# Image pipeline with attention: two buffers of normalised sums, three tiles divided after turning, and another order of maxima, projection and loads

## The reference

```python
# layer 0, per image and channel
x = x + relu(-median(x))                       # median over the 16384 pixels
y = relu(upfirdn2d(x, lpf, up=2))              # 7 taps, zero padded
x = upfirdn2d(y, lpf, down=2)
# layer 1
spec = rfft2(x)                                # gate from |spec|: two 1x1 maps, gelu, sigmoid
xf = x + irfft2(spec * gate)
q = xf @ q_w + q_b                             # 4 heads of 16, 16384 queries
k, v = keys and values of two strided convolutions of xf (8x8: 256 keys, 16x16: 64 keys),
       layer norm, kv map, v by a 3x3 depthwise convolution
out = softmax(q k^T / 4) v                     # 320 keys
result = out @ proj_w + proj_b + x
```

## Time and profile before

| | us |
|---|---|
| median of 3 runs | 10953.36 (10936.6 to 10957.42) |
| the profiled execution's own time | 10947.25 |
| its span, from the first to the last instruction | 10945.9 |
| busy: PE, weight loads, DVE, ACT, POOL | 9935.8, 4884.1, 8640.6, 7155.3, 5880.3 |

### The profile page before, as it was taken

How to read it: one execution, slowest core, us unless ns; L and a number is a source line. 1 busy time by engine, 2 the same in 40 slices (tenths; PEclk the granted TensorE clock), 3 DMA queues, 4 the chain that set the end, 5 groups by cost and what they waited for, 6 DMA issues and landing times. The chain is left out here.

```text
span 10945.9 us, 199054 instructions
## 1 busy us (share of the span) xinstructions
PE 9935.8 (91%) x69001; PEld 4884.1 (45%) x69001; DVE 8640.6 (79%) x14529; ACT 7155.3 (65%) x12301; POOL 5880.3 (54%) x10577
## 2 busy tenths in 40 slices
PE   1998998989989899899989999899898998989989
PEld 1534535344353543535435353453534435354353
DVE  7887778878788777878777788777887878877787
ACT  5766667666666766667666676666667666676665
POOL 1374463745637365472744737446374553836547
PEclk9999999999999999999999999999999999999999
DMA  2031231312314032140322303123131331413214
GB/s 61 29 77 51 56 90 30 79 40 65 81 33 90 27 76 70 41 90 36 73 55 51 96 23 80 46 59 87 32 79 37 68 79 34 90 33 72 67 44 102
DMA packets 330611, 664.69 MB, mean 61 GB/s; under 512 B 95624, under 2 KB 241160, under 8 KB 308048
## 3 DMA queue, kind: packets, MB, share of 16 engines
q1 hardware_dynamic: 329552, 651.29, 25.1%
HBM read 232.53 MB, written 71.30 MB: 28 GB/s over the span
## 5 line engine op out<-in xcount | busy, mean ns | idle before, releaser
L1350 ACT ACTIVATE R<-ps 128x512 f32<-128x512 f32 x5120 | 2874.0, 593 | 1460.9 <-PE ps L826 1020.6
L1117 DVE TENSOR_REDUCE R<-ps 128x2 f32<-128x640 f32 x3840 | 3028.3, 818 | 725.7 <-PE ps L805 682.1
L269 ACT ACTIVATE R<-R,st 128x1475 bf16<-128x1475 f32 (+2 forms) x1326 | 2014.4, 1519 | 441.5 <-DVE st L343 416.3
L332 DVE TENSOR_SCALAR_CACHE_REDUCE R<-R,st 128x1255 bf16<-128x1255 f32 (+2 forms) x1326 | 2015.1, 1520 | 19.5 <-DVE st L343 0.2
L805 PE MATMUL ps<-KST,R 96*128 96x320 bf16 x7680 | 1683.2, 300 | 42.9 <-DMA R<-R 21.6
L851 PE MATMUL ps<-R 128*32 128x512 f32 x12288 | 1670.1, 617 | 0.0
L826 PE MATMUL ps<-R,KST 104*128 104x512 bf16 x4096 | 1583.2, 389 | 11.4 <-ACT R L1350 6.8
L1447 POOL TENSOR_TENSOR R<-R 128x256 f32<-128x256 f32 x1440 | 1056.9, 734 | 115.2
L1451 POOL TENSOR_TENSOR R<-R 128x256 f32<-128x256 f32 x1440 | 1050.2, 729 | 119.9
L805 PEld LDWEIGHTS ps<-KST,R 96*128 96x128 bf16 x7680 | 703.0, 98 | 752.6 <-DVE R L1117 280.0
L826 PEld LDWEIGHTS ps<-R,KST 104*128 104x128 bf16 x4096 | 394.6, 97 | 1043.8 <-ACT R L1350 749.6
(11 more groups left out here) (226 smaller groups left out, 19536.4 us busy)
## 6 DMA issues: line engine op xcount, KB each, us to landing
R<-R SPq DMA_DIRECT2D x3072, 64.0 KB, 2.4
R<-xh_in SPq DMA_DIRECT2D x136, 512.0 KB, 4.5
out_dram<-Z SPq DMA_DIRECT2D x68, 1024.0 KB, 3.9
R<-Wk SPq DMA_DIRECT2D x960, 64.0 KB, 2.0
Wk<-Wk SPq DMA_DIRECT2D x960, 64.0 KB, 2.0
R<-xa_in SPq DMA_DIRECT2D x36, 1024.0 KB, 10.1
R<-xb_in SPq DMA_DIRECT2D x36, 1024.0 KB, 11.7
R<-sr_in SPq DMA_DIRECT2D x32, 1024.0 KB, 5.0
```

The costliest lines, as they stand in the source:

```text
L269: e.activation(junka[:, 2047:2048] if k == LONE else junka[:, 0:o2 - o1], xc[:, o1:o2], ACT.Sign, bias=mid, scale=-1.0, accum_out=ca[i]).t ...
L332: e.tensor_scalar(junk[:, 0:o1 - o0], xc[:, o0:o1], mid, None, ALU.is_le, ALU.add, accum_out=cv[i]).then_inc(md_cv, 1)
L1117: e.tensor_reduce(MX[(4 * u + s4) % 2][:, blk_, h0:h0 + 2], ps[:, 2 + 2 * bq:4 + 2 * bq, 0:320], axis=AX.X, op=ALU.max).then_inc(mx, 1)
L1350: e.activation(PB[:, t % 2, w, :], ps[:, w % 2, :], ACT.Exp).then_inc(ex, 1)
```

## The change

- STAGES moves the stages from slots 2 and 6 to slots 4 and 8, or from 2 to 4.
- The normalised sums get two buffers NO[0] and NO[1] of their own. `normalise` runs for tiles 0 to 28, and waits only for its own last result and for the projection of the tile two back. The turned sums ON and OX move to another place.
- TURNED = 3: tiles 29, 30 and 31 are divided after turning. The turning of tile 29 lies inside tile 31 (turn after slot 1, turn_back after slot 6).
- `project_out` is for tile t - 4, in slot 0; `rest` follows in slot 2.
- `split_max` is in slot 2 of the tile in whose slot 3 `lay_max` turns the maxima (they were in slot 8 of the tile before, and slot 0).
- SP: lay_out comes first, for tile t - 2; `load_next` is cut in two parts, in tiles 28 and 29; two loads of a unit come ahead of lay_max and the others behind it; the units 2 and 3 are loaded by eight DMAs in a tile, one unit after the other.
- VectorE's reductions of the next image (`largest`, L305) move to the slots 4 and 6 of tile 31.

```diff
@@ -21,11 +21,13 @@
 WAITS = 4
 AHEAD = 2
 WEIGHS = (2, 4, 8)
-STAGES = {(0, 2): (1, 0, 6), (0, 6): (1, 1, 6), (1, 2): (1, 2, 6), (1, 6): (1, 3, 6),
-          **{(8 * g - 12 + j, 2): (g, j, 6) for g in (2, 3) for j in range(4)}}
+STAGES = {(0, 4): (1, 0, 6), (0, 8): (1, 1, 6), (1, 4): (1, 2, 6), (1, 8): (1, 3, 6),
+          **{(8 * g - 12 + j, 4): (g, j, 6) for g in (2, 3) for j in range(4)}}
 ADDS = {17: (0,), 19: (1,), 21: (2,), 23: (3,), 25: (4,), 27: (5,), 31: (6, 7)}
 FIRST = [(0, i) for i in range(11)] + [(1, 0), (1, 1)] + [(0, i) for i in range(11, 16)] + [(1, 2), (1, 3)]
-LOADS = {u: 2 if u == 2 else 4 * u - 8 for u in range(2, 8)}
+LOADS = {**{3 * u - 4 + i: (u, 8 * i, 8 * i + 8) for u in (2, 3) for i in range(3)},
+         **{4 * u - 8 + i: (u, 6 * i, 6 * i + 6) for u in range(4, 8) for i in range(4)}}
+TURNED = 3
 NP = 3
 CUTS = [HALF * i // NP for i in range(NP + 1)]
 LONE = 20
@@ -154,7 +156,8 @@
         OR = [W[:, 512 * i:512 * i + 512] for i in range(2)]
         XO = [W[:, 1024 + 256 * i:1280 + 256 * i] for i in range(2)]
         XD = [R2[:, 1024 + 256 * i:1280 + 256 * i] for i in range(2)]
-        XI, XN2, ON, OX = (R2[:, 1536 + 256 * i:1792 + 256 * i] for i in range(4))
+        XI, XN2, *NO = (R2[:, 1536 + 256 * i:1792 + 256 * i] for i in range(4))
+        ON, OX = W[:, 1536:1792], W[:, 1792:2048]
         RD = [R2[:, 2640 + 16 * i:2656 + 16 * i] for i in range(2)]
         RS = [W[:, 1536 + 512 * i:2048 + 512 * i] for i in range(2)]
...
 
 
 
-        def load_next(e, it, half, landed=None):
+        def load_next(e, it, half, landed=None, part=None):
             src = (xa, xb)[half][bass.ds(it, 1), :, :, :].rearrange("a c t n -> (a t) c n")
+            a, b = (0, 4096) if part is None else (2048 * part, 2048 * part + 2048)
             for t in range(2):
-                e.dma_start(xc[64 * t:64 * t + 64, 4096 * half:4096 * half + 4096], src[t, :, :]).then_inc(landed or in_xc[half], 16)
+                e.dma_start(xc[64 * t:64 * t + 64, 4096 * half + a:4096 * half + b], src[t, :, a:b]).then_inc(landed or in_xc[half], 16)
 
         def load_image(e, it, k):
...
                 for i in range(2):
-                    op = e.matmul(ps[:, 6, 128 * i:128 * i + 128], lhsT=XN2[:, 128 * i:128 * i + 128], rhs=c("pw"),
+                    op = e.matmul(ps[:, 6, 128 * i:128 * i + 128], lhsT=NO[t % 2][:, 128 * i:128 * i + 128], rhs=c("pw"),
                                   start=True, stop=True)
                 op.then_inc(po_ps, 1)
...
@@ -870,13 +874,13 @@
                 op.then_inc(den_ps, 1)
 
             def turn_back(t):
-                e.wait_ge(od, t - NT + 3)
+                e.wait_ge(od, t - NT + TURNED + 1)
                 for i in range(2):
                     op = e.transpose(ps[:, 4 + t % 2, 128 * i:128 * i + 128], ON[:, 128 * i:128 * i + 128], c("ident"))
                 op.then_inc(ot_ps, 1)
 
             def project_back(t):
-                e.wait_ge(ox, t - NT + 3)
+                e.wait_ge(ox, t - NT + TURNED + 1)
                 e.wait_ge(*b6[0])
                 for i in range(2):
                     op = e.matmul(ps[:, 6, 128 * i:128 * i + 128], lhsT=OX[:, 128 * i:128 * i + 128], rhs=c("pw"),
@@ -897,19 +901,24 @@
                         values()
                     if w < 8 and ahead < NT:
                         maxima(ahead // 4, ahead % 4, w)
-                    if w == (0 if t else 4) and t + AHEAD - 1 < NT:
+                    if w == 0 and t > 3:
+                        project_out(t - 4)
+                    if w == 3 and t + AHEAD - 1 < NT:
                         lay_max(t + AHEAD - 1)
                     if w in WEIGHS and t:
                         weigh(t - 1, WEIGHS.index(w))
-                    if w == 5 and t > 2:
-                        project_out(t - 3)
                     if (t, w) in STAGES:
                         stage(*STAGES[t, w])
-            e.wait_ge(mx, 8 * NT - 16)
+                    if t == NT - 1 and w == 1:
+                        e.wait_ge(mx, 8 * NT - 16)
+                        turn(NT - 3)
+                    if t == NT - 1 and w == 6:
+                        turn_back(NT - 3)
+            project_out(NT - 4)
             turn(NT - 2)
             weigh(NT - 1, 0)
+            project_back(NT - 3)
             weigh(NT - 1, 1)
-            project_out(NT - 3)
             turn_back(NT - 2)
             weigh(NT - 1, 2)
             project_back(NT - 2)
...
 
             def sums(t):
                 e.wait_ge(pv_ps, t + 1)
-                if t > 1:
+                if t == NT - 1:
+                    e.wait_ge(den_ps, 1)
+                elif t > 1:
                     e.wait_ge(in_o[t % 2], 64 * (t // 2))
                 e.tensor_copy(OR[t % 2], ps[:, 7, :]).then_inc(ou, 1)
 
...
                 heads = ps[:, 2 + t % 2, :].rearrange("p (a d s) -> p a d s", a=16, s=2)
-                n = t - NT + 3
+                n = t - NT + TURNED + 1
                 e.wait_ge(den_ps, n)
                 e.reciprocal(RD[t % 2], heads[:, :, 0, 1]).then_inc(rc, 1)
...
@@ -1151,21 +1162,24 @@
             for t in range(NT):
                 u, s4, ahead = t // 4, t % 4, t + AHEAD
                 for w in range(10):
-                    if w == 7 and t > 2:
-                        rest(t - 3, True)
+                    if w == 2 and t and t + AHEAD - 1 < NT:
+                        split_max(t + AHEAD - 1)
+                    if w == 2 and t > 3:
+                        rest(t - 4, True)
                     if w < 8 and ahead < NT:
                         maxima(ahead // 4, ahead % 4, w)
-                    if w == 8 and ahead < NT:
-                        split_max(ahead)
                     if w == 8 and t:
                         sums(t - 1)
-                    if t == NT - 1 and w in (1, 4):
-                        e.wait_ge(in_xc[0], 32)
-                        largest(e, w // 4)
+                    if t == NT - 1 and w == 3:
+                        divide(NT - 3)
+                    if t == NT - 1 and w in (4, 6):
+                        e.wait_ge(in_xc[0], 64)
+                        largest(e, w // 2 - 2)
                     if divmod(10 * t + w - 1, 10) in STAGES:
                         stage(*STAGES[divmod(10 * t + w - 1, 10)])
+            rest(NT - 4, True)
             divide(NT - 2)
-            rest(NT - 3, True)
+            rest(NT - 3, False)
             sums(NT - 1)
             rest(NT - 2, False)
             divide(NT - 1)
@@ -1328,6 +1342,13 @@
                     e.wait_ge(in_m[t % 2], 16 * (t // 2))
                 e.activation(MR[t % 2], pb[0:8, :], ACT.Copy).then_inc(mr, 1)
 
+            def turned(t):
+                n = t - NT + TURNED
+                e.wait_ge(ot_ps, n + 1)
+                if n:
+                    e.wait_ge(po_ps, t)
+                e.activation(OX, ps[:, 4 + t % 2, 0:256], ACT.Copy).then_inc(ox, 1)
+
             def values():
                 e.wait_ge(va_ps, 1)
...
                     e.activation(PB[:, t % 2, w, :], ps[:, w % 2, :], ACT.Exp).then_inc(ex, 1)
-                    if w == (1 if t else 4) and t + AHEAD - 1 < NT:
+                    if w == 3 and t + AHEAD - 1 < NT:
                         lay_max(t + AHEAD - 1)
                     if t == 0 and w == 8:
                         values()
                     if (t, w) in STAGES:
                         stage(*STAGES[t, w])
-            for n in range(2):
-                e.wait_ge(ot_ps, n + 1)
-                if n:
-                    e.wait_ge(po_ps, NT - 2 + n)
-                e.activation(OX, ps[:, 4 + n, 0:256], ACT.Copy).then_inc(ox, 1)
+                    if t == NT - 1 and w == 7:
+                        turned(NT - 3)
+            turned(NT - 2)
+            turned(NT - 1)
 
 
 
...
                 if t:
-                    e.wait_ge(po_ps, t)
+                    e.wait_ge(on, t)
+                if t > 1:
+                    e.wait_ge(po_ps, t - 1)
                 e.tensor_scalar(XI.bitcast(I32), XD[k].bitcast(I32), -1.0, NEAR, ALU.mult, ALU.add).then_inc(nt, 1)
                 for _ in range(3):
                     e.wait_ge(nt, n + 1)
...
-                e.tensor_tensor(XN2, XO[k], XI, ALU.mult).then_inc(on, 1)
+                e.tensor_tensor(NO[k], XO[k], XI, ALU.mult).then_inc(on, 1)
 
             for j in range(4):
...
                         stage(*STAGES[t, w])
-                    if w == 4 and t > 1:
+                    if w == 4 and 1 < t < NT - TURNED + 2:
                         normalise(t - 2)
                     if w == 9 and t in ADDS:
...
@@ -1531,8 +1553,11 @@
             lay_max(0)
             for t in range(NT):
                 u, s4 = t // 4, t % 4
-                if t + AHEAD - 1 < NT:
-                    lay_max(t + AHEAD - 1)
+                if 1 < t < NT - TURNED + 2:
+                    lay_out(e, t - 2)
+                if t >= NT - 4 and t < NT - 2:
+                    e.wait_ge(sc_ps, 280)
```

(18 more changed lines are left out.)

## The result

The changed kernel took 11056.97 us (median of four runs, 11043.8 to 11065.26); the kernel before, on the same chip, 10946.15 (10936.6 to 10957.42). The ratio is 1.0106, with 1.0093 to 1.0119 as its interval: slower by 111 us, where 35 fewer were forecast. The number is close to that of the first rival (11062).

A forecast was written before the change was run, and what follows sets the result against it. TensorE's own order was taken to set the pace in mid-loop, with losses in waits elsewhere. The terms summed to -2.2 us an image, -35 in all, from 10953 to 10918 us; 8-in-10 range 10840 to 11045.

The forecast's parts named there:

- the first rival: Tiles 20 to 28, even: GpSimd's add_median runs between the split's halves; +9 us an image, 11062 in all; chance 0.2.
- The middle, +0.28 a tile: Middle of the attention loop: reordered TensorE slots lengthen each of 26 tiles by 0.28 us, +7.3 an image.
- The 0.06 for a split behind a product of the division (1.5): Middle of the loop: split waits for GpSimd's division beyond spare time, 0.06 us a tile, +1.5 an image.
- Tiles with a stage: Eight loop tiles with a stage: no term of their own, only the middle's +0.28 us a tile.
- Tiles 0 to 3: Loop start: tiles 1 to 3 lack a projection to fill slot 0; +0.8 us an image, between -1 and +3.
- Tile 6, -2.0: Tile 6: the DMA wait for unit 2 disappears as one unit is loaded at a time; -2.0 us an image.
- Tiles 8, 16 and the odd ones from 19, -2.9: Tiles 8, 16, 19 to 29: late-split stalls (-2.4) and projection waits for GpSimd (-0.5) go; -2.9 us an image.
- The added wait, +2.6 at tile 29's start: Tile 29's scores wait for lay_max, issued in tile 28 behind half the load; +2.6 us an image, bounds 0 and 5.
- The end, -9.5: Loop end, from tile 30's scores to the last addition: TensorE's division waits go; -9.5 us an image, between 6 and 11.
- the second (the middle loses nothing): Middle of the loop: VectorE's spare time moves to slots 5 to 7, no loss; -141 us more, 10777; chance 0.12.
- The third: Tiles 16 to 19 and 24 to 27: lay_max late behind loads, 1 us each; +128 us, 11046; chance 0.08.
- The fourth: Loop end doesn't come back: the replacement chain is as long, 4.5 of 9.5 stay; +72 us, 10990; chance 0.1.

The follow-up runs named there:

- experiment 1: The changed kernel with add_median inside the division, behind its first instruction instead of its last: 10923.15 us, ratio 0.998.
- experiment 2: The changed kernel with VectorE's split of the maxima in slot 1 instead of slot 2: 10905.78 us, ratio 0.9964.
- experiment 4: The changed kernel with maxima, split, projection and stages back in the old kernel's slots; also called the fourth kernel: 10813.22 us, ratio 0.9877.
- experiment 7: The kernel before the change, with only units 2 and 3 loaded one after the other, eight DMAs a tile: 10905.57 us, ratio 0.9969.
- Experiment 3: The changed kernel with SP issuing the halves of load_next in tiles 28 and 29 behind lay_max: 11008.41 us, ratio 1.0063.
- in after: "After" is the changed kernel itself, measured against the kernel before: 11056.97 us, ratio 1.0106.
- experiment 5: experiment 4's kernel with lay_max issued on SP right behind lay_out, ahead of all loads; also called the fifth kernel: 10747.39 us, ratio 0.9824.
- experiment 6: experiment 5's kernel with add_median inside the division too: 10742.55 us, ratio 0.9818.
- experiment 9: The kernel before the change, with the uncut 2 MB load_next issued in tile 28 behind lay_out: 11004.88 us, ratio 1.0051.

## Why the prediction was wrong, step by step

**The step that failed is the first rival's chance.** The sum has nothing for L1088's wait behind add_median, the rival gave it 9 us an image at a chance of 0.2, and it measured 9.2. Its mechanism was written down in full, with the point that decides: whether the division's last product starts before or after 2.4 us, with 2.1 as the value worked out. In tile 22 that product started at 2.14 us (818.70 - 816.56) and the split at 2.38; the split ended at 4.76, where the rival said 4.8. By the rule that the rival itself stated, 2.1 before 2.4 means the stall. I forecast the other way, since the phase is a sum of five durations and 0.3 us seemed thin. But a thin margin on the wrong side is no argument for the right side. (The start of the division, 0.5 + 1.8 + 2.0, adds up to 4.3 and not the 4.4 written, so the margin was rather 0.4.) The phase does wander, but seldom far enough: in the tiles 22 to 28 the product started at 1.84 to 2.25 us with the split at 2.38, and all 64 were hit; in tile 20 it started at 1.83 to 2.89, and the ten below 2.38 were hit and the six above were not. The price was right as well: the five tiles cost 10.5 us an image more than before, less 1.35 for the middle's 0.27 each, 9.2 for the 9 given. Experiments 1 and 2, which take it away from either engine's side, give back 134 and 151 (of which some 24 are no part of the stall). The first gives back 7.8 an image in the loop and not 9.2, since the stall had hidden the wait for lay_max at tile 29's start. What the Trainium skill (SBUF — State Buffer, Who interferes with whom) says, that of a VectorE instruction with two SBUF inputs and a GpSimd one that reads SBUF the second to issue fully blocks, agrees with the 1.82 us. The prediction had quoted that rule, and its own rows had shown it with a shorter partner.

That the rival's total comes within 5 us of the measured 11057 is partly luck: the other terms are off by 4.2 us an image one way and 4.6 the other. The prediction's chances add up to 0.14 and 0.38 where it has 0.15 within and 0.37 slower; nothing hangs on that.

Term by term, per image:
- *The middle, +0.28 a tile*: +0.27 in tiles 9 to 11, with slots 5 to 7 at 1.96 as forecast; experiment 4 takes it back (8.91). Right. The 0.06 for a split behind a product of the division (1.5) was not there on top: in tile 10 L1095 took 0.47 us, and the tile's 9.18 is 0.29 over 8.89; with the split in slot 1 (experiment 2) the tiles 9 to 11 are no shorter.
- *Tiles with a stage*: +0.52 in eight tiles (0.43 to 0.55), where the same 0.28 was put. Mis-sized, by 2.0. With the old slots they are back at 9.84 (experiment 4). With the split in slot 1 they last 10.18 (experiment 2), which leaves +0.33: most of the excess goes with the split's slot 2, where its first half waits behind a product of the division.
- *Tiles 0 to 3*: +1.26 for 0.8, within its bounds; tile 1 alone has +1.22.
- *Tile 6, -2.0*: -2.1, once the stage's 0.55 is taken out (11.94 to 10.40), and experiment 7 gives 2.1 alone. Right.
- *Tiles 8, 16 and the odd ones from 19, -2.9*: these came down by 2.1 against the middle's 0.27. Right but for 0.8. The tiles 17 and 18 cost 0.3 together beyond the middle.
- *The added wait, +2.6 at tile 29's start*: it came one tile later, 1.25 to 2.2 us at tile 30's, since tile 28 was lengthened by the stall and covered its own. Without the stall (experiment 1) it stands where it was forecast, with 1.3 to 1.75 us. Tile 29 costs 1.3 more than the middle. Experiment 3 removes it.
- *The end, -9.5*: -8.9, with 24.8 us in the first image for 24.6 forecast. Right. Another 1.4 came back before the next image's loop.

From -2.2 to +6.6 are 8.8: the rival 9.2, the stages 2.0, tiles 0 to 3 0.5, the stalls 0.8, the tiles 17 and 18 0.3 and the end 0.6 more; the middle with the stall of the split 1.8 less, tile 6 0.1 less, the added wait 1.3 less, the stretch between the images 1.4 less: 8.8.

Of the other rivals, the second (the middle loses nothing) falls by tiles 9 to 11. The third came true in its first four tiles where the maxima are turned in slot 0 (experiment 4), and in after by 0.4 us an image. The fourth falls: the end came back.

The new slots together cost 244 us by the medians (experiment 4), and 232 between the two profiled executions. Of these 232, by the tile lengths, the tiles 20 to 28 with the stall have 127, the eight with a stage 69, the tiles 0 to 3 21 and 8 to 11 19, and tile 29, the end and the stretch between the images 15 together; less 19 in the tiles 16 to 19, where turning in slot 3 hides most of the wait for lay_max's DMA. What the change brings without its slots, once lay_max is first on the queue, is experiment 5: -194 us against before.

## What to carry to other kernels

Where instructions of two engines exclude each other, work out in which order their queues reach the point, and forecast by the side on which the worked-out phase falls, even with a margin of 0.3 us: here it fell on that side in 74 of 80 cases. Two small dependent instructions of one engine are two chances for the other engine's longest instruction to come between; move the short ones to another slot, or put the long one inside a chain that is not late. Either can cost elsewhere: with the split in its old slot, add_median inside the division made the loop 24 us longer (experiment 6). And when a big load is moved behind one small transfer, look which small transfer is next on the queue and how soon its reader needs it.

## What the runs showed of the hardware

- VectorE's L1095, started while GpSimd's L1476 ran, ended 0.04 us behind it; its successor L1097 (both 128x16, two inputs in SBUF), started 0.11 us behind an instruction that GpSimd had ready (L401, 128x1024), ended 0.04 us behind that one: 1.82 us for 0.18. GpSimd's L401 took 1.89 us, its median in this run. So two dependent instructions in a row were each held up, by different partners. In experiment 3, tile 20, the last product started at 1.5 to 1.6 us in four images and was over before the split; there the first half was held up by add_median and took 1.73 to 1.85 us.
- On SP's queue a small transfer behind 1 MB made its reader wait 1.25 to 2.2 us (after, tile 30), behind 2 MB 7.5 to 8.2 (experiment 9). The Trainium skill (DMA: Bandwidth & Descriptors, Queues, rings and completion order) says that each DMA engine consumes its descriptors in ring order; the trace agrees, with 11.8 us from lay_max's issue to the scores that it released.
- The stretch between the last addition and the next image's loop lasts 347.9, about 350 or about 352 us from image to image in after, with the same instructions. The granted clock is at half (1.2 for 2.4 GHz) for 30.7 us of the shortest, 30.7 to 37.5 of the middle ones and 37.5 to 41.0 of the longest. In the fifth kernel all fifteen take 351.5 to 351.9 with 37.5 at half, in the fourth most take 349.6 to 349.8 with 30.7: 28 us in all, though nothing there was edited. What decides it stays open, and so a difference of under 30 us between two kernels can't be put down to an edit by the totals alone.
